# GpSimd's splits of the second weight block wait for the last low parts of the dense layer's input

## The chip, the cores and the metric

The kernel runs on one core of one Trainium2 chip. The metric is device time in microseconds (us) of one launch. In this text PE (TensorE) multiplies matrices, DVE (VectorE) and ACT (ScalarE) read its results from PSUM, POOL (GpSimd) works in SBUF only, and SP (SyncE) issues most of the DMAs. Each engine works through its own list of instructions in order, and waits on semaphores.

## The reference, cut to what matters

Four layers work on 4 x 256 tokens of 256 numbers, each followed by a residual sum and a layer norm: an mLSTM attention, a mixture of 16 experts of which each token takes 4, a gated linear attention (GLA) and a mixture of 32 experts of which each token takes 8. The change lies between the third and the fourth.

```python
x = _layernorm(x + _L1_attn_ref(x, ...))          # GLA, ends with silu(gproj) * o @ Wo.T
x = _layernorm(x + _L1_ffn_ref(x, ...))
# _L1_ffn_ref: routing and then every expert on every token
logits = x @ gate_weight.T
probs = softmax(logits); topv, topi = top_k(probs, 8)
...                                               # thresholds, then combine[token, expert]
gu = x @ w_gu.T; g, u = split(gu, 2)
acc = acc + (silu(g) * u) @ w_d.T * c_e[:, None]
```

## The kernel before

Products in full precision are made of three passes: each operand is split into a high part (a rounded copy) and a low part (the rest), and PE adds high times high, high times low and low times high (`mm3`, L1970). Tokens lie in 8 tiles of 128 (`NT`); two tiles share a PSUM bank, so there are 4 pairs.

**The dense layer.** The fourth layer computes all 32 experts for all tokens, in 8 blocks of 4 experts (`quad_slot(q)`). A block has six steps (`step_of`): two halves of 512 tokens, three chunks of 128 rows each. In a step PE makes the gate and the up product, 6 matmuls of 512 columns each (`gate_up`, L2299); ACT applies silu to the first (L1047) and in steps 0 to 5 copies the second to SBUF (L1052); the product of the two is made by POOL in steps 0 to 5 (`mixed`, L880) and by DVE later (L1677). Ten steps behind, POOL multiplies by the routing weights (L889), ACT and DVE split the product (L1070, L1682), and PE multiplies it by the down weights.

**The weights.** SP loads the gate, up and down weights of a block; POOL splits them: `high` (L811) and `low` (L816). Block 0 is split between the state products of GLA. Block 1 has its four splits in one piece after the last state product: a high and a low part of 1536 columns, then a high and a low part of 768 columns for the down weights. The first pair raises `gate_split` to 2, the second `down_split` to 2. They stand ahead of the six `mixed` products in POOL's list. PE needs `gate_split` 2 for step 6. SP waits for both before it loads block 3 (L589, L595), and after that for the routing weights.

**The input.** `lo_done` counts pairs whose low parts are written, four per layer. Its values 9 to 12 are the pairs of GLA's output before the projection `Wo` (`lo_parts`, L1549). Values 13 to 16 are the pairs of the normed sum, which is the dense layer's own input (`layernorm_by_halves`, DVE L1553, ACT L1005): per half of four tiles the statistics (L1559, L1567), `rv` = variance plus epsilon (L1569) and its reciprocal (L1570), ACT's root (L1010), the scaled tiles (DVE L1579, ACT L1013), four transposes per pair by PE (`turn_half`, L2247), the high parts by ACT (L1019) and the low parts by DVE (L1588).

**Where the routing stands.** PE begins step 0 with the first half's input (L2290, L2295), turns the second half, makes the router's products between the pieces of step 1 (L2256), and turns the logits (L2264). DVE then runs softmax, the eight best, the thresholds and the combine weights CW (`softmax` L1603, `route1` L1633, `combine` L1649) as one chain of some thirty small instructions from L1607 to L1665. PE turns CW (`turn_weights`, L2328) between steps 5 and 6, and step 7 waits until CW has been copied out of PSUM.

Around the change `AHEAD` is 6, and ACT's silu of step i waits for `mixed` of step i - 2, since both use two buffers:

```python
if 2 <= i < AHEAD + 2:
    act.wait_ge(mixed_pool, i - 1)
```

Of the kernel before, what the change touches and what calls it, by code (L numbers as in the profile page):

```python
# [28 lines left out]
def build_kernel(nc, a, out):  # L29
# [3 lines left out]
    NT = T // P  # L33
# [29 lines left out]
    with ExitStack() as ctx:  # L63
# [3 lines left out]
        def sem(name):  # L67
            return ctx.enter_context(nc.semaphore(name))
# [270 lines left out]
        lo_done = sem("lo_done")  # L339
# [147 lines left out]
        def quad_slot(q):  # L487


            n, c = GCOLS, DCOLS  # L490
            if q % 2 == 0:
                return [flat(EG[:])[:, 0:n], EW4[:, 0:n], EW4[:, n:2 * n],
                        flat(ED[:])[:, 0:c], EW4[:, 2 * n:2 * n + c], EW4[:, 2 * n + c:2 * n + 2 * c]]
            return [FA[:, 0:n], RA[:, 0:n], RA[:, n:2 * n],
                    FA[:, GLA_WORDS:GLA_WORDS + c], RA[:, 2 * n:2 * n + c], flat(W1H[:])[:, 0:c]]
# [52 lines left out]
        def _(sp):  # L548
# [15 lines left out]
            def load_expert(e, par):  # L564

                land_g, _, _, land_d, _, _ = MOE.slot(par)
                sp.dma_start(land_g.rearrange("p (k c) -> p k c", k=KD),
                             a["gateup0"][bass.ds(e, 1)].rearrange("o (k p) i -> p (o k) i", p=P)
                             ).then_inc(ld_exp[par], 16)
                sp.dma_start(land_d.rearrange("p (c d) -> p c d", d=D),  # L570
                             a["down0"][bass.ds(e, 1)].rearrange("o (c p) d -> p (o c) d", p=MOE.IP)
                             ).then_inc(ld_exp[par], 16)
# [68 lines left out]
        def _(pool):  # L641
# [195 lines left out]
                    low(dl, d, dh, whole, d_rounded).then_inc(down_split, 1)  # L837

            g, gh, gl, d, dh, dl = quad_slot(1)
            pool.wait_ge(lo_done, 3 * (NT // 2))  # L840
            pool.wait_ge(gate_ld[1], 32 * KD)
            g_rounded = high(gh, g, whole)
            low(gl, g, gh, whole, g_rounded).then_inc(gate_split, 1)
# [1119 lines left out]
        def _(pe):  # L1963
# [315 lines left out]
            def moe_pe():  # L2279

                def gate_up_first():

                    b = step_bank(0)
                    _, gh, gl, _, _, _ = quad_slot(0)
                    pe.wait_ge(gate_split, 1)
                    pe.wait_ge(hi_done, 3 * (NT // 2) + 2)
                    for up in range(2):
                        for k, (xh, _) in enumerate(xm(0)):
                            for j, g in enumerate((gh, gl)):
                                pe.matmul(bank(b + up), chunk_of(g, k, up, 0), xh, start=(k == 0 and j == 0), stop=False,  # L2290
                                          skip_group_check=True)
                    pe.wait_ge(lo_done, 3 * (NT // 2) + 2)
                    for up in range(2):
                        for k, (_, xl) in enumerate(xm(0)):
                            ins = pe.matmul(bank(b + up), chunk_of(gh, k, up, 0), xl, start=False, stop=(k == KD - 1),  # L2295
                                            skip_group_check=True)
                        ins.then_inc(gate_up_mm, 1)
# [382 lines left out]
```

## Time and profile before

| | us |
|---|---|
| median of 3 runs (lowest, highest) | 591.24 (590.7, 593.32) |
| the profiled execution | 589.8 |
| its span, first to last instruction | 588.0 |
| PE busy in the span | 523.6 (89%) |
| DVE, ACT, POOL busy | 327.0, 230.5, 348.8 |

The mean granted clock of TensorE in the span is 0.948 of full speed. A row of a timeline gives start, duration, engine, line, operation, the tiles written and read, and in brackets the idle time of the engine ahead of it with what ended it. Rows of one line that follow each other are merged (x4 is four instructions). A duration includes the time in which an instruction that has been started can't go on. L numbers are lines of the kernel.

### The profile page before, as it was taken

The numbers are of one execution on the slowest core, as the hardware profiler recorded it, in microseconds if no ns is written. First come the engines' busy times: TensorE is split into PE (matmuls) and PEld (weight loads), VectorE is DVE, ScalarE is ACT, GpSimd is POOL, SyncE is SP. The second block draws the span as 40 slices with busy tenths as digits, with TensorE's granted clock in tenths as the row PEclk, the third lists the DMA queues.
The fourth block names the chain that finished last, engine by engine and source line by source line (L and its number), as shares of the span: only waits on it lengthen the run. The fifth ranks groups of instructions, "written<-read, shape, count | busy, mean of one in ns | idle before, by whom it ended". The sixth has DMA issues, their size and how long they took to land.

```text
span 588.0 us, 9553 instructions
## 1 busy us (share of the span) xinstructions
PE 523.6 (89%) x3033; PEld 426.0 (72%) x3035; DVE 327.0 (56%) x726; ACT 230.5 (39%) x539; POOL 348.8 (59%) x316
## 2 busy tenths in 40 slices
PE   7999986339998999988989768999999999999994
PEld 4766666329887989966645438778888888888884
DVE  4635688634666444435998958563333252433276
ACT  3555542315554766545502022663232323232334
POOL 3394012777998797671377824254947657698180
PEclk9979998759998999999989968899999999999999
DMA  8999983245675766543000050204234343144022
GB/s 249 365 386 386 349 296 132 101 137 173 201 245 175 208 188 180 172 124 107 1 1 1 0 161 3 80 10 141 74 107 121 114 143 99 36 135 140 5 72 71
DMA packets 72864, 83.69 MB, mean 142 GB/s; under 512 B 7617, under 2 KB 63698, under 8 KB 72818
## 3 DMA queue, kind: packets, MB, share of 16 engines
q1 hardware_dynamic: 33490, 38.90, 22.0%
q10 hardware_dynamic: 35968, 35.26, 17.9%
q0 software_dynamic: 3360, 8.93, 4.9%
q8 instruction: 26, 0.43, 0.3%
q14 instruction: 20, 0.16, 0.1%
HBM read 48.61 MB, written 34.47 MB: 141 GB/s over the span
## 4 chain that ended last, share of the span: by engine, by line
PE 61%; DVE 14%; DMA 5%; issue 5%; POOL 4%; ACT 2%; ACTq 0%; DVEq 0%; POOLq 0%
PE PS L1970 47%; DMA FA<-xg 4%; POOL xg L708 3%; DVE FA L1923 2%; DVE PS L1904 2%; PE PS L2376 2%; PE PS L2495 2%; PE PS L2045 1%; PE PS L2067 1%; PE PS L2400 1%; PE PS L2507 1%; DVE HC L1378 1%; DMA FA<-yg,tix 1%; POOL FA L783 1%; PE PS L2192 1%
## 5 line engine op out<-in xcount | busy, mean ns | idle before, releaser
L1970 PE MATMUL PS<-XH,EW 128*128 128x512 f32 x392 | 129.8, 395 | 0.2 <-DVE EW L1278 0.2
L1677 DVE TENSOR_TENSOR FA<-OGATE,PS 128x512 f32<-128x512 f32 x42 | 28.9, 688 | 108.8 <-ACT OGATE L1047 90.7
L1970 PEld LDWEIGHTS PS<-XH,EW 128*128 128x128 f32 x392 | 73.7, 188 | 16.3 <-DVE EW L1278 0.7
L1970 PE MATMUL PS<-EW,XH 128*128 (+2 forms) x252 | 77.0, 389 | 3.6 <-issue 2.2
L1047 ACT ACTIVATE OGATE<-PS 128x512 f32<-128x512 f32 x48 | 28.7, 599 | 124.1 <-PE PS L1970 124.1
L1970 PE MATMUL PS<-XL,EW 128*128 128x512 f32 x196 | 77.0, 393 | 0.0
L1970 PE MATMUL PS<-EW 128*128 128x256 f32 x288 | 63.2, 284 | 0.6 <-DVE W1L L1682 0.4
L824 POOL TENSOR_TENSOR FA<-FA,QT 128x1024 f32<-128x1024 f32 (+1 forms) x16 | 37.4, 2338 | 32.5 <-DVE FA L1923 32.5
L1970 PE MATMUL PS<-EW,W1L 128*128 128x256 f32 x192 | 54.3, 283 | 0.0
L1970 PEld LDWEIGHTS PS<-EW 128*128 128x128 f32 x288 | 49.1, 189 | 4.2 <-DVE W1L L1682 1.5
L1970 PEld LDWEIGHTS PS<-EW,XH 128*128 128x128 f32 x252 | 44.8, 198 | 8.3 <-issue 2.8
L1682 DVE TENSOR_TENSOR W1L<-FA,EW 128x512 fp32r<-128x512 f32 x48 | 46.6, 978 | 2.8 <-ACT EW L1070 2.8
L1970 PE MATMUL PS<-EW,XL 128*128 (+2 forms) x126 | 46.6, 370 | 0.0
L889 POOL TENSOR_TENSOR FA<-FA,HC 128x512 f32<-128x512 f32 x24 | 34.5, 1442 | 16.7 <-DMA HC<-cw_room 16.7
L708 POOL DMA_INDIRECT xg<-XB,tix x32 | 31.3, 978 | 19.4 <-DVE tix L1463 10.4
L889 POOL TENSOR_TENSOR FA<-FA,QT 128x512 f32<-128x512 f32 x24 | 34.2, 1433 | 14.2 <-DMA QT<-cw_room 14.2
L1970 PEld LDWEIGHTS PS<-XL,EW 128*128 128x128 f32 x196 | 37.0, 189 | 6.8
L1970 PE MATMUL PS<-EW,EHH 112*128 x188 | 40.2, 306 | 0.1
L1923 DVE TENSOR_TENSOR_SCAN FA<-FA,PS 128x1024 f32<-128x1024 f32 x16 | 36.6, 2286 | 0.5
L1782 DVE TENSOR_TENSOR XL<-PS,XH 128x256 fp32r<-128x256 f32 x47 | 19.9, 424 | 30.0 <-ACT XH L1114 29.7
L1793 DVE TENSOR_TENSOR SQ<-SIL,PS 128x224 f32<-128x224 f32 x47 | 18.2, 388 | 32.7 <-ACT SIL L1133 32.2
L1970 PEld LDWEIGHTS PS<-EW,W1L 128*128 128x128 f32 x192 | 36.3, 189 | 0.0
(395 smaller groups left out, 1210.7 us busy)
## 6 DMA issues: line engine op xcount, KB each, us to landing
xg<-EQ ACTq DMA_DIRECT2D x1, 16384.0 KB, 60.7
EG<-in_gateup SPq DMA_DIRECT2D x16, 448.0 KB, 4.0
yg<-EQ ACTq DMA_DIRECT2D x1, 6016.0 KB, 19.7
FA<-xg ACTq DMA_DIRECT2D x47, 128.0 KB, 2.2
yg<-FA ACTq DMA_DIRECT2D x47, 128.0 KB, 2.6
ED<-in_down SPq DMA_DIRECT2D x16, 224.0 KB, 4.5
EG<-in_gateup SPq DMA_DIRECT2D x16, 192.0 KB, 3.0
FA<-in_gateup SPq DMA_DIRECT2D x16, 192.0 KB, 3.2
```

Of the source, the lines that this page charges most:

```text
L708: pool.indirect_dma_start(out=xg, out_offset=bass.IndirectOffsetOnAxis(ap=slots[:, n:n + 1], axis=0), in_=XB[:, t, :], in_offset=None).the ...
L824: pool.tensor_tensor(QS[:, v % 2, c], STATE[:, v % 2, c], QT[:, c], ALU.mult).then_inc(qs_done, 1)
L889: pool.tensor_tensor(mixed[:, v % MIXED, :], mixed[:, v % MIXED, :], spread_w[v % SPREADS], ALU.mult).then_inc(weighted, 1)
L1047: act.activation(sil_t[:, i % 2, :], bank(b), ACT.Silu).then_inc(sil_done, 1)
L1677: dve.tensor_tensor(mixed[:, i % MIXED, :], sil_t[:, i % 2, :], bank(step_bank(i) + 1), ALU.mult).then_inc(mixed_dve, 1)
L1682: dve.tensor_tensor(h_lo[:, v % TURNED, :], mixed[:, v % MIXED, :], h_hi[:, v % TURNED, :].bitcast(F32), ALU.subtract).then_inc(h_lo_done, 1)
L1782: dve.tensor_tensor(XL[:, :, c], bank(2 + i % 2)[:, 0:D].rearrange("p (k c) -> p k c", k=KD), XH[:, :, c].bitcast(F32), ALU.subtract).then ...
L1793: dve.tensor_tensor(HH[:, i % 2, 0:I], SIL[:, i % 2, 0:I], bank(i % 2)[:, I:2 * I], ALU.mult).then_inc(sh_ready, 1)
L1904: dve.tensor_tensor(spread_v(v), KT, spread_v(v), ALU.mult).then_inc(d1_done, 1)
L1923: dve.tensor_tensor_scan(STATE[:, v % 2, :], DEC, spread_v(v), 0.0, ALU.mult, ALU.add).then_inc(s_done, 1)
L1970: ins = pe.matmul(o, l, r, start=start and i == 0, stop=stop and i == n - 1, skip_group_check=True)
L2376: ins = pe.transpose(bank(2 + i % 2)[:, k * P:(k + 1) * P], XG[:, i % 4, k * P:(k + 1) * P], ident[:])
```

## The change

One number in POOL's list changes: the wait ahead of block 1's splits. Every engine has the same instructions in the same order as before.

```diff
@@ -837,7 +837,7 @@
                     low(dl, d, dh, whole, d_rounded).then_inc(down_split, 1)
 
             g, gh, gl, d, dh, dl = quad_slot(1)
-            pool.wait_ge(lo_done, 3 * (NT // 2))
+            pool.wait_ge(lo_done, 4 * (NT // 2))
             pool.wait_ge(gate_ld[1], 32 * KD)
             g_rounded = high(gh, g, whole)
             low(gl, g, gh, whole, g_rounded).then_inc(gate_split, 1)
```

`3 * (NT // 2)` is 12, the last pair of GLA's output; `4 * (NT // 2)` is 16, the last pair of the dense layer's input.

## Rows read from the trace of the kernel before

**Rows 1.** Chain of waits, 340 to 420 us: start, us, engine, tile, line

```profile
363.88 2.10 DVE rv L1569
...
380.48 0.70 DVE LG L1607
...
391.87 1.05 PE PS L2328 x8
392.91 27.17 PE PS L1970 x137
```

**Rows 2.** Timeline of POOL, 290 to 405 us

```profile
360.89 1.48 POOL L811 TENSOR_SCALAR EW<-FA 128x1536 fp32r<-128x1536 f32 x1 [16.48 <-DVE XL L1549]
362.46 3.49 POOL L816 TENSOR_TENSOR EW<-FA,EW 128x1536 fp32r<-128x1536 f32 x1
...
366.83 1.81 POOL L816 TENSOR_TENSOR W1H<-FA,EW 128x768 fp32r<-128x768 f32 x1
379.66 2.56 POOL L880 TENSOR_TENSOR FA<-OGATE 128x512 f32<-128x512 f32 x2 [11.01 <-ACT OGATE L1052]
385.58 1.29 POOL L880 TENSOR_TENSOR FA<-OGATE 128x512 f32<-128x512 f32 x1 [3.36 <-ACT OGATE L1052]
387.07 1.29 POOL L880 TENSOR_TENSOR FA<-OGATE 128x512 f32<-128x512 f32 x1 [0.21 <-ACT OGATE L1052]
```

**Rows 3.** Timeline of DVE, 370 to 425 us

```profile
370.84 0.17 DVE L1569 TENSOR_SCALAR rv<-mv 128x4 f32<-128x4 f32 x1
...
375.39 1.42 DVE L1588 TENSOR_TENSOR XL<-PS,XH 128x256 fp32r<-128x256 f32 x4 [2.82 <-ACT XH L1019]
...
381.21 0.42 DVE L1610 TENSOR_REDUCE rsum<-LG 128x8 f32<-128x256 f32 x1
...
385.13 0.22 DVE L1635 TENSOR_TENSOR t<-t,alpha 128x64 f32<-128x64 f32 x1
...
385.65 1.31 DVE L1637 TENSOR_TENSOR t<-t,rsum 128x64 f32<-128x64 f32 x1
...
387.50 0.88 DVE L1642 SCALAR_TENSOR_TENSOR rbest<-rsum,rbest 128x8 f32<-128x8 f32 x1
```

**Rows 4.** Timelines of DVE and POOL later in the dense layer, 414 to 420 us

```profile
414.39 2.54 POOL L889 TENSOR_TENSOR FA<-FA,HC 128x512 f32<-128x512 f32 x2
...
415.99 1.49 DVE L1682 TENSOR_TENSOR W1L<-FA,EW 128x512 fp32r<-128x512 f32 x1
416.90 2.29 POOL L816 TENSOR_TENSOR EW<-FA,EW 128x768 fp32r<-128x768 f32 x1
```

**Rows 5.** Timeline of PE, 345 to 425 us

```profile
367.81 1.06 PE L2247 MATMUL PS<-ident,XB 128*128 128x128 f32 x8 [1.89 <-DVE XB L1579]
369.70 3.30 PE L2290 MATMUL PS<-XH,EW 128*128 128x512 f32 x8 [0.83 <-ACT XH L1019]
...
380.37 0.50 PE L1970 MATMUL PS<-XH,EW 128*128 128x512 f32 x1
...
391.39 0.39 PE L1970 MATMUL PS<-XH,EW 128*128 128x512 f32 x1
```

**Rows 6.** Windows: length, busy of five engines, TensorE's granted clock, DMA share, GB/s

```profile
182.50:189.30 6.80, 4.64 (x20) 4.36 (x21) 4.09 (x8) 1.93 (x6) 4.88 (x7) 0.75 0.51 161
325.80:332.60 6.80, 4.28 (x18) 1.54 (x17) 6.73 (x5) 0.00 (x0) 5.29 (x4) 1.00 0.00 0
...
366.80:373.60 6.80, 4.96 (x18) 3.97 (x19) 5.32 (x19) 4.19 (x8) 1.81 (x1) 0.75 0.60 174
```

**Rows 7.** Timeline of ACT, 370 to 425 us

```profile
372.74 1.28 ACT L903 ACT_TABLE_LOAD   x1
...
374.75 1.09 ACT L1019 ACTIVATE XH<-PS 128x512 fp32r<-128x512 f32 x2 [0.52 <-PE PS L2247]
...
384.37 0.58 ACT L1047 ACTIVATE OGATE<-PS 128x512 f32<-128x512 f32 x1
```

**Rows 8.** Timeline of SP's DMA issues, 340 to 420 us

```profile
365.98 2.50 SPq L589 DMA_DIRECT2D FA<-in_gateup  x4
```

## The prediction

> **What bounds the kernel now.** I read the page first: PE is busy for 89% of the span. Then the chain of waits over the end of GLA and the start of the dense layer. From 392.9 us on it is one row of 137 matmuls and stays on PE [rows 1]. So what counts is the time at which PE can go on from the turned routing weights, 391.87. Whatever moves that instant moves the end by as much, and a wait in the front of the chain counts only as far as it reaches it.
>
> Ahead of it the chain goes through two pieces of DVE. The first is the layer norm of the first half: `rv` (L1569), four numbers per partition, takes 2.10 us [rows 1], and its twin for the second half 0.17 [rows 3]. The timeline of POOL shows what stands beside it: the low split of block 1, 362.46 plus 3.49, ends at 365.95, and `rv` ends at 365.97 [rows 1, 2]. DVE waited for the end of a POOL instruction. The second piece is the routing chain, L1607 at 380.48 to CW, ready just ahead of 391.87. It shows the same three times: L1637 takes 1.31 us where L1635, of the same form, takes 0.22, and ends at 386.96, beside a POOL product that ends at 386.87; L1642 takes 0.88 and ends at 388.38, beside one that ends at 388.36 [rows 2, 3]; L1611 in the same way waits for the end of the pair of products from 379.66. These three hold some 1.1, 0.7 and 0.4, together 2.2 us. L1610, a reduction of one tensor, runs in 0.42 in the middle of a POOL product and isn't held [rows 2, 3]. So instructions of DVE that read two tensors from SBUF, and small ones like `rv`, are held to the end of POOL's current instruction; reads of PSUM and reductions are not.
>
> PE itself was nearly as late as CW: its last matmul of step 5 starts at 391.39 and its turn of CW at 391.87, so 0.2 us were spare [rows 1, 5]. Both arms have to get shorter for a gain.
>
> **The change, step 1: the stall goes.** POOL is then silent from GLA's last product until the last low part. `rv` falls from 2.10 to 0.17, which is 1.9 us on the chain. PE waited 1.89 for that half's tiles ahead of 367.81 [rows 5], so it can take all of it and start turning at some 365.9.
>
> **Step 2: the clock.** In the 6.8 us from 366.8 on the granted clock averages 0.75: half of the stretch is at 1.2 GHz [rows 6]. The 8 matmuls of step 0 take 3.30 us there. At 2.4 GHz the 48 matmuls of steps 2 to 5 start over 391.39 - 380.37 = 11.02 us, 0.234 each [rows 5], so eight take 1.9. Ahead of the fall PE stood still for 1.89 and 0.83 us; the first of the two goes. I take it that the clock then stays up here, worth 1.4 for the 8 and some 0.3 for the 4 after them. Not all arrives: ACT's table load ends at 374.02, and its high part at 374.75, which had waited 0.52 for PE, comes behind it [rows 7]. That row can move by 1.9 for the stall and by 0.5 for the wait at most, to 372.3. The last low part, at 376.81 before [rows 3], keeps its distance of 2.1 and comes at 374.4. From there PE has 4 router matmuls and 6 of step 1, 10 x 0.234 = 2.3, and the turn of the logits, eight small transposes, for which I take 0.7 (the eight of CW's turn take 1.05 [rows 1]): L1607 starts at 377.5 in place of 380.48, a lead of 3.0 us. If the clock falls all the same, the lead is 1.9.
>
> **Step 3: the splits now stand in front of the routing chain.** Before they took 360.89 to 368.64, 7.75 us [rows 2]. Now: high part 374.4 to 375.9, low part to 379.5, the down weights' high part to 380.3, their low part to 382.2. Queued behind them are the six products. The first began at 379.66 before [rows 2]; now it can't begin before 382.2, so the first two run to 383.5 and 384.8. ACT's silu of step 2 waits for the first of them. It ran at 384.37 before, late because of the routing's table loads [rows 7], now at 383.6. PE's step 4 waits for that silu: it would be there at 377.4 + 24 x 0.234 = 383.0 and starts at 384.2. It still reaches the turn of CW at 384.2 + 24 x 0.234 = 389.8, 1.8 ahead of before.
>
> DVE's chain is worse off, because POOL is now busy without a gap from 374.4 to 384.8 and then nearly without. I walk it with the durations of before and hold each two-tensor instruction to the end of the POOL instruction then running: L1611 waits 0.5 (low part), L1620 0.6 (down low), L1623 0.9 (first product), L1635 1.1 (second), L1637 0.8 (third), L1639 1.1 (fourth), L1642 1.1 (fifth), L1663 0.2 (sixth): 6.3 us in place of 2.2. One DVE instruction goes in between two POOL instructions in a row: L1682 started inside a pair of POOL products, and took 1.49 until 417.48; the POOL instruction after the pair then took 2.29 [rows 4] where the same form takes 1.81 [rows 2]. If DVE had no turn in between, the chain would wait for a gap in POOL's work, up to 2 us more. The nearest row says that it gets its turn, and I take that. What holds eight instructions up is a matter of tenths: an instruction ready just ahead of POOL's next one isn't held at all, and each such escape gives 0.8 to 1.1 back.
>
> CW's instant: 391.87 - 3.0 (lead) + 6.3 - 2.2 (holds) = 393.0, **1.1 us later than before**. PE, there at 389.8, stands still for some 3 us.
>
> The Trainium skill, "SBUF — State Buffer", section "SBUF: two separate sides", says that GpSimd and a VectorE instruction that uses both its read ports share one pair of ports as an exclusive lock: whoever starts first has it for the whole instruction, the other fully blocks. The holds above agree. No row here has the eight MAX8 of L1614 beside POOL; by that page's rule they, with one input, aren't held, and the sum stays; if they were, a part of 0.8 would be added.
>
> **Step 4: PE's pause.** Two stretches that held a pause lost half their clock: 182.5 to 189.3, busy 4.64 of 6.80, and 366.8 to 373.6. A third, 325.8 to 332.6, busy 4.28, kept it [rows 6]. A single pause of 3 us with PE busy to both sides is closest to the first. I give the fall 6 in 10 where PE waits so long, at the price of the stretch at 370: 1.4 us. Bounds: 0 and 1.7.
>
> **Other edges.** PE needs the split for step 6, after 392.9; it is done at 379.5. SP's loads of block 3, issued at 365.98 before, start at 379.5 and end near 383; its next work waits for the copy of CW, which PE turns at 391.87 before, so that costs nothing [rows 1, 8]. The cover is some 9 us thick. POOL's sixth product follows PE's step 5 as before.
>
> **The sum.** +1.1 (CW) + 1.4 (clock) = +2.5 us on the profiled execution, 589.8 to 592.3. That execution lies 1.4 under the median of the runs; on the median it is 593.7, or 0.4% up: by that less than the 0.5% which a measurement of this kernel can tell from no change.
>
> **The rivals.**
> A. The same, and the clock stays up at 390: +1.1, 592.3. For it: the third stretch of [rows 6].
> B. The chain slips through. Holds stay near the 2.2 of before, since ready times fall into POOL's seams; then CW leads, PE's arm decides, 391.6 to 389.8, -1.8 us: 589.4. Against it: POOL has hardly a seam before 384.8. Over 0.5% faster would take -3, which not even PE's arm gives.
> C. Slower: the clock still falls at 370, so the lead is 1.9 and not 3.0. The last low part comes at 374.9, the splits end at 382.7, CW at 391.87 - 1.9 + 4.1 = 394.1, +2.2, or +1.4 if the later start spares L1611 and L1639 a part of their holds; with the fall after it +3.6: 594.8. It decides from a CW over 1.6 later than before together with the fall.
> D. The stall of `rv` has nothing to do with POOL: no lead, all the holds: +4.1, 595.3. The coinciding ends speak against it.
>
> **How the numbers follow.** Forecast 0.42, A 0.22, B 0.16, C 0.16, D 0.04. The likeliest is 593.7. Its own spread is some 1 us, so a quarter of its chance (0.10) lies beyond 594.2, where 0.5% ends; with C's larger part and D that makes slower 0.26. Faster by 0.5% needs under 588.3: 0.04, from B. Within: 0.70. The range takes in B's centre and C's: 589.4 to 595.2.
>
> **What the profile of the changed kernel would show.** Right: the first `rv` at some 0.17; the splits from 374.4; granted clock 1.0 from 366 to 374; L1607 at about 377.5; a silu of step 2 released by POOL's product; L1620 to L1642 at about 1 us each; PE's idle time ahead of L2328 near 3 us with DVE named, and a stretch at half clock behind it. Wrong: `rv` still long (step 1), half clock at 370 (step 2), L1607 to L1665 hardly longer than the 11.3 of before (step 3), full clock after the pause (step 4).

## The result, and the profile after

| | before | changed |
|---|---|---|
| median us (lowest, highest) | 589.49 (584.18, 596.59), 20 runs | 593.84 (587.5, 598.59), 20 runs |
| the profiled execution | 589.8 | 587.76 |

The ratio is 1.0066, with an interval of 1.0039 to 1.0092: 0.7% slower, by some 3.9 us. The medians are of all 20 runs, while the ratio leaves out runs over 1.5% above the fastest of their kernel, of which the changed kernel has 3. Timed a second time beside the experiments the ratio was 1.0057 (1.0023 to 1.009). The profiled execution of the changed kernel is one of the fastest of its 20, so its span of 585.9 against 588.0 says nothing by itself. Clock and history ahead of this place differ between executions by several us. So all instants below that are called "from L1355" count from the start of DVE's instruction L1355, the first of the norm inside GLA. It lies 9.7 us ahead of the splits of the kernel before, the first thing that the change moves. In these two executions it starts at 351.21 and 347.67.

The timeline of DVE before, and that of the changed kernel:

```profile
351.21 0.29 DVE L1355 TENSOR_SCALAR hs<-PS 128x128 f32<-128x128 f32 x1 [3.35 <-PE PS L2547]
...
381.66 0.84 DVE L1611 TENSOR_TENSOR LG<-LG,rsum 128x256 f32<-128x256 f32 x1
382.98 0.85 DVE L1614 MAX8 top<-PR 128x8 f32<-128x32 f32 x8 [0.48 <-ACT PR L1034]
...
391.39 0.42 DVE L1665 TENSOR_TENSOR CW<-CW,rsum 128x256 f32<-128x256 f32 x1
```

```profile
347.67 0.29 DVE L1355 TENSOR_SCALAR hs<-PS 128x128 f32<-128x128 f32 x1 [3.35 <-PE PS L2547]
...
360.34 0.17 DVE L1569 TENSOR_SCALAR rv<-mv 128x4 f32<-128x4 f32 x1
...
373.85 0.69 DVE L1607 TENSOR_REDUCE LG<-PS 128x256 f32<-128x512 f32 x1 [3.27 <-PE PS L2264]
...
375.03 0.96 DVE L1611 TENSOR_TENSOR LG<-LG,rsum 128x256 f32<-128x256 f32 x1
376.48 0.85 DVE L1614 MAX8 top<-PR 128x8 f32<-128x32 f32 x8 [0.48 <-ACT PR L1034]
...
377.93 0.71 DVE L1620 SCALAR_TENSOR_TENSOR rv<-rsum,rbest 128x8 f32<-128x8 f32 x1
...
378.91 1.03 DVE L1623 TENSOR_TENSOR t<-top,rsum 128x64 f32<-128x64 f32 x1
379.97 1.19 DVE L1635 TENSOR_TENSOR t<-t,alpha 128x64 f32<-128x64 f32 x1
...
381.45 1.09 DVE L1637 TENSOR_TENSOR t<-t,rsum 128x64 f32<-128x64 f32 x1
382.58 0.23 DVE L1639 TENSOR_TENSOR t<-t,first 128x64 f32<-128x64 f32 x1
...
383.10 0.88 DVE L1642 SCALAR_TENSOR_TENSOR rbest<-rsum,rbest 128x8 f32<-128x8 f32 x1
...
384.54 1.27 DVE L1647 TENSOR_TENSOR t<-top,t 128x64 f32<-128x64 f32 x1
...
387.53 1.25 DVE L1663 SCALAR_TENSOR_TENSOR CW<-HC,PR 128x256 f32<-128x256 f32 x1
388.81 0.93 DVE L1665 TENSOR_TENSOR CW<-CW,rsum 128x256 f32<-128x256 f32 x1
```

The stall of the first `rv` is gone: 0.17 in place of the 2.10 of [rows 1]. L1607 starts 26.2 from L1355, against 29.3 in [rows 1]. From there on the chain loses what it had won. L1623 and L1635 take over 1 us each; [rows 3] has L1635 with POOL idle, 0.22. An instruction is called held here where it takes longer than its form does with POOL idle: 0.42 for two inputs of 128x256, 0.22 for 128x64, 0.17 for 128x8. Nine instructions are held, together 6.8 us. Before it was 2.3, of which three instructions (L1611, L1637, L1642) make 2.2. CW is ready at 42.1 from L1355 in place of 40.6.

The timelines of POOL and ACT in the changed kernel show what stands beside the chain:

```profile
370.66 1.47 POOL L811 TENSOR_SCALAR EW<-FA 128x1536 fp32r<-128x1536 f32 x1 [28.92 <-DVE XL L1588]
372.22 3.49 POOL L816 TENSOR_TENSOR EW<-FA,EW 128x1536 fp32r<-128x1536 f32 x1
...
376.77 1.84 POOL L816 TENSOR_TENSOR W1H<-FA,EW 128x768 fp32r<-128x768 f32 x1
378.57 3.90 POOL L880 TENSOR_TENSOR FA<-OGATE 128x512 f32<-128x512 f32 x3
382.67 1.29 POOL L880 TENSOR_TENSOR FA<-OGATE 128x512 f32<-128x512 f32 x1 [0.20 <-ACT OGATE L1052]
```

```profile
379.95 0.60 ACT L1047 ACTIVATE OGATE<-PS 128x512 f32<-128x512 f32 x1 [1.99 <-POOL FA L880]
```

The splits follow the last low part, and three products follow the splits without a gap; before, the first two products stood alone and the third came 3.4 us later [rows 2]. ACT's silu of step 2 now waits 1.99 for a product of POOL. The timeline of PE in the changed kernel:

```profile
364.11 2.11 PE L2290 MATMUL PS<-XH,EW 128*128 128x512 f32 x8 [0.83 <-ACT XH L1019]
```

```profile
380.60 0.50 PE L1970 MATMUL PS<-XH,EW 128*128 128x512 f32 x1 [0.99 <-ACT OGATE L1047]
...
386.06 0.40 PE L1970 MATMUL PS<-XH,EW 128*128 128x512 f32 x1
...
389.80 1.05 PE L2328 MATMUL PS<-ident,CW 128*32 128x128 f32 x8 [3.33 <-DVE CW L1665]
```

The eight matmuls of step 0 run at full clock, 2.11 us for the 3.30 of [rows 5]. Step 4 waits 0.99 for the silu. And PE, done with step 5, stands still for 3.5 us until CW is there; before it hardly waited. The 3.5 counts from 386.3, when a next matmul could have started (0.23 behind the last one); the 3.33 in the brackets counts from the recorded end of the last one. All pauses of PE below are counted in the first way, except where brackets are named.

From the turn of CW (the start of L2328) to the end, called the tail below, it is 196.10 us in this execution and 196.13 in that of before. So between these two executions all the difference in this part is the instant of the turn: 42.13 from L1355 against 40.66. That makes the changed kernel 1.5 us slower here; its span is shorter all the same, because L1355 starts 3.5 us earlier in this execution.

### The profile page after: what moved, and what is told of

The parts are those of the page before. It is cut to its first block, busy times and chain, and to the rows that moved or that the text cites. A ratio compares the mean times of both kernels' runs of the same rounds, so it can differ in the third digit from the quotient of the medians.

```text
span 585.9 us, 9553 instructions
## 1 busy us (share of the span) xinstructions
PE 520.2 (89%) x3033; PEld 421.4 (72%) x3035; DVE 329.3 (56%) x726; ACT 230.3 (39%) x539; POOL 348.1 (59%) x316
## 4 chain that ended last, share of the span: by engine, by line
PE 56%; DVE 14%; POOL 6%; DMA 6%; issue 4%; ACT 3%; POOLq 1%; ACTq 0%; SPq 0%; DVEq 0%
PE PS L1970 44%; DVE FA L1923 3%; DMA FA<-xg 2%; DMA FA<-yg,tix 2%; DVE PS L1904 2%; POOL FA L783 2%; DMA ED<-in_down 2%; POOL xg L708 2%; PE PS L2495 1%; PE PS L2045 1%; PE PS L2067 1%; PE PS L2376 1%; PE PS L2507 1%; PE PS L2400 1%; POOL EW L752 1%
## 5 line engine op out<-in xcount | busy, mean ns | idle before, releaser
L811 POOL TENSOR_SCALAR EW<-FA 128x768 fp32r<-128x768 f32 (+1 forms) x11 | 11.2, 1027 | 50.4 <-DVE XL L1588 28.9
L1970 PE MATMUL PS<-EW,EHH 112*128 x188 | 39.6, 303 | 0.1
```

The lines of the kernel that those rows point to most:

```text
L1970: ins = pe.matmul(o, l, r, start=start and i == 0, stop=stop and i == n - 1, skip_group_check=True)
```

## The experiments

Each diff below is against the changed kernel. Two theories stood against each other at first. H: the loss is made by POOL's splits ahead of the routing chain (a later CW), and by the clock, which falls in some executions after PE's pause. R: it comes from elsewhere (the wait itself, the later loads of block 3, or something that every kernel with a silent POOL would pay). The profiled instants are a sharper measure than the medians here, whose intervals are some 0.3% wide to each side.

| kernel | turn of CW from L1355 | turn to end | holds | ratio to before |
|---|---|---|---|---|
| before, three profiles | 40.66, 39.60, 39.60 | 196.1, 196.3, 196.4 | 2.3 | 1 |
| changed, four profiles | 42.13, 42.15, 42.15, 42.17 | 196.1, 199.1, 198.0, 196.4 | 6.8 | 1.0066, 1.0057 |
| pause filled (e2) | 42.12 | 196.3 | 6.8 | 1.0054 |
| gate pair early, down pair at the last low part (e3) | 39.92 | 198.0 | 4.6 | 0.9985 |
| splits of 16 columns (e4) | 37.57 | 196.2 | 2.3 | 0.9987 |
| all splits at the scaled tiles (e5) | 39.95 | 198.0 | 4.6 | 1.0018 |
| gate pair early, down pair at the scaled tiles (e6, e8) | 37.57, 37.61 | 196.4, 196.1 | 2.3 | 0.9978, 0.9959 |
| gate pair as before, down pair late (e7) | 39.75 | 196.1 | 2.6 | one run |

### The changed kernel three times more (e1, c1, c2)

No edit.

> The changed kernel again, beside the kernels of this set. Theory H (holds and clock): CW, the combine weights, is ready about 1.5 us later than before; PE pauses about 3.3 us ahead of turning it (L2328), and in a part of the executions the clock falls to 1.2 GHz after the pause, some 1.4 us more. Ratio to before 1.003 to 1.007. Rival N (the first count of runs was noise, and the profiled execution, 2 us faster than that of before, is typical): ratio 0.997 to 1.001.

> The changed kernel, a third profile, for what varies between its executions. Theory H: CW turned at 42.1 after L1355 as in the first two; the time from there to the end 196.1 to 196.4 if the clock stays up, 198 to 199.1 if it falls at the pause of 3.5 us; I expect the fall in more than half of the executions. Rival (the fall of the second profile was an exception): 196.1 to 196.4.

> The changed kernel, a fourth profile, with the same two outcomes: 42.1 to the turn, then 198 to 199.1 with a fall of the clock at the pause (theory H, more than half of the executions) or 196.1 to 196.4 (rival).

Measured: 1.0057 (1.0023 to 1.009), so N, that the first count of runs was noise, falls. The turn stands at 42.1 to 42.2 in all four profiles; it is no accident of one execution. What varies is the tail. In two of four it is 196.1 and 196.4, in c1 198.0, in e1 199.1. The timelines of e1, DVE and then PE, and its windows (length, busy of five engines, granted clock, DMA share, GB/s):

```profile
348.28 0.29 DVE L1355 TENSOR_SCALAR hs<-PS 128x128 f32<-128x128 f32 x1 [1.72 <-PE PS L2547]
```

```profile
390.43 1.89 PE L2328 MATMUL PS<-ident,CW 128*32 128x128 f32 x8 [3.34 <-DVE CW L1665]
```

```profile
384.00:388.00 4.00, 3.10 (x14) 2.19 (x12) 3.86 (x23) 2.75 (x6) 2.06 (x3) 1.00 0.00 0
388.00:392.00 4.00, 1.57 (x9) 1.10 (x9) 2.31 (x3) 0.22 (x1) 3.92 (x3) 0.67 0.00 0
392.00:396.00 4.00, 4.00 (x12) 3.12 (x11) 0.68 (x1) 1.18 (x2) 0.04 (x1) 0.50 0.15 33
396.00:400.00 4.00, 4.00 (x18) 3.26 (x17) 0.87 (x2) 0.60 (x1) 1.65 (x2) 0.98 0.62 186
```

PE had been at full clock and mostly busy until 387, then paused; the clock falls to 1.2 GHz still within the pause and stays there for 6.8 us. The turn of CW takes 1.89 in place of 1.05, and the tail is 2.9 us longer. In c1 the low stretch lasts 3.4 us and costs 1.7. The fall came in 2 of 4 executions where I had expected more than half.

### PE's pause filled (e2)

```diff
-                    pe.wait_ge(cw_step, CW_READY)
                     pe.wait_ge(sil_done, AHEAD - 1)
                     pe.wait_ge(up_copied, AHEAD - 1)
+                    keep_warm(12, 2)
+                    pe.wait_ge(cw_step, CW_READY)
```

> The changed kernel, with 12 matmuls on zeros (128x512 bf16, bank 2, which the turned weights overwrite) ahead of PE's wait for CW, so that PE is busy for some 2.6 of the 3.3 us of its pause. CW's time is not touched. Theory H: what is left is the later CW, +1.5 us or less; the share of the clock goes, so ratio 1.000 to 1.003, below the changed kernel of this set by 1 to 2.5 us. Rival C (the clock plays no part, all of the loss is the later CW): same as the changed kernel within 0.5 us.

The timeline of PE in e2:

```profile
389.81 2.54 PE L1992 MATMUL PS<-zb 128*128 128x512 bf16 x11
393.08 1.05 PE L2329 MATMUL PS<-ident,CW 128*32 128x128 f32 x8 [0.73 <-DVE CW L1665]
```

The idle time ahead of the turn shrinks to 0.73, the clock stays up, the turn is where it was. The times don't decide: 1.0054 (1.0025 to 1.0083) against 1.0057 for the changed kernel in the same set. The medians are 592.3 and 592.95 us, 0.65 apart, where each interval is 1.7 to 2 us wide to each side. So the fall of the clock is shown by profiles, its share in the median is not shown by this run. And 1.0054 is more than the 1.5 us that I had left for the later CW. That contradiction led to the next question: is the profile of before typical?

### The kernel before twice more (b1, b2)

No edit.

> The kernel before, a second profile, to see which parts of the first one vary between executions. Theory P (where the clock stays up at 370 us in that kernel, CW is turned earlier): rv about 2.1, CW turned at 40.7 after L1355 if the clock falls there, and 39.5 to 40.2 if it doesn't. Rival: 40.7 in both.

> The kernel before, a third profile, with the same question: 40.7 after a fall of the clock at 370 us, 39.5 to 40.2 without one (theory P), or 40.7 in both.

The timelines of DVE and PE in b1:

```profile
350.27 0.29 DVE L1355 TENSOR_SCALAR hs<-PS 128x128 f32<-128x128 f32 x1 [3.35 <-PE PS L2547]
...
378.48 0.69 DVE L1607 TENSOR_REDUCE LG<-PS 128x256 f32<-128x512 f32 x1 [3.27 <-PE PS L2264]
```

```profile
389.87 1.05 PE L2328 MATMUL PS<-ident,CW 128*32 128x128 f32 x8
```

L1607 stands at 28.2 and the turn at 39.6, in both; the clock stayed up around 370. Theory P holds: the half clock of [rows 6] at 366.8 to 373.6 is there in one of three executions and costs 1.1 us. The change therefore moves CW from a usual 39.6 to 42.1, by 2.5 us, not by 1.5. With the tails of e1 and c1 (2.9 and 1.7, none in two, so 1.1 on the average) and 0.4 for the one execution of before in three that was late, this gives 2.5 + 1.1 - 0.4 = 3.2 us, against 3.4 to 3.9 measured. The averages are of four profiles and of three, so this agreement is rough. With e2's tail it gives 2.1, or 1.0036, inside its interval.

### Splits of 16 columns (e4)

```diff
+            bit = lambda w: w[:, 0:16]
-            g_rounded = high(gh, g, whole)
-            low(gl, g, gh, whole, g_rounded).then_inc(gate_split, 1)
+            g_rounded = high(gh, g, bit)
+            low(gl, g, gh, bit, g_rounded).then_inc(gate_split, 1)
...
```

> The changed kernel with the four splits of block 1 cut to 16 columns each: the waits and counts stay, POOL's 7.8 us of work go (so the weights of block 1 are left unsplit, a part of the computation that this kernel leaves out). Theory H: lead of 3.0 at L1607, holds of 2 to 2.5 us in the routing chain, CW about 2.5 to 3 us earlier than before, PE's pause under 0.5: ratio 0.994 to 0.996. Rival R: the wait itself, or the loads of block 3 that start later, cost the time: ratio 1.003 or more as in the changed kernel.

This kernel leaves out the splits of the other columns of block 1, so its result is not that of the reference. The turn of CW stands at 37.57, 4.6 us ahead of the changed kernel, with the wait as it is there. The holds are 2.3, those of before, and PE has no pause. So the wait by itself costs nothing, and the 7.8 us of splits in that place make all of the 4.5 us of additional holds. SP's loads of block 3 are not quite where the changed kernel has them: they are issued 23.5 us from L1355, against 28.1 there and 14.8 before. That the later loads cost nothing is shown by the time from the turn to the end, 196.1 in the changed kernel with its loads latest of all, and 196.2 here. So theory R falls for the wait and for the loads. The ratio, 0.9987 (0.995 to 1.0024), has its middle above the 0.994 to 0.996 expected. These had been counted from the late profile of before; the turn is 2.0 us ahead of a usual one, which is 0.9966, inside the interval.

### The gate pair early, the down pair late (e3)

```diff
             g, gh, gl, d, dh, dl = quad_slot(1)
-            pool.wait_ge(lo_done, 4 * (NT // 2))
+            pool.wait_ge(gated, 2 * NT)
             pool.wait_ge(gate_ld[1], 32 * KD)
...
+            pool.wait_ge(lo_done, 4 * (NT // 2))
             pool.wait_ge(down_ld[1], 16)
```

> The splits are parted: the gate pair (high and low, 5.1 us) starts as soon as DVE has scaled GLA's output (16 more counts of gated), about 2.8 us earlier than before, so that it ends ahead of the first rv (L1569); the down pair (2.7 us) waits for the last low part, as in the changed kernel. Theory H: rv 0.17 us, the second rv and L1607 lead as in the changed kernel (2.7 to 3.1 us ahead of before), the down pair ends ahead of the first product of POOL that ACT needs, the holds in the routing chain fall back to 2 to 3.5 us in place of 6.9, CW 1.5 to 3 us earlier than before, PE's pause under 0.5 us: ratio 0.994 to 0.998. Rival R (what made the changed kernel slower is not the splits' place ahead of the routing chain): ratio 1.002 or more. A third outcome: the gate pair is itself slowed or slows DVE's last scaling, rv still waits: ratio 1.000.

The first `rv` takes 0.17 and L1607 comes at 26.2, as expected; CW doesn't: the turn is at 39.9, just where a usual execution of before has it. The down pair itself is over at 25.75 from L1355, ahead of the chain. But POOL's first two products queue behind it and start 0.37 us later than in e6 (below), at 25.72 against 25.35. The second of them holds L1611 (L1612 in these kernels) by 0.36 us more. That alone shifts the chain by 0.36, and L1658, near its end, then starts 0.03 us behind the start of a POOL product that it escapes in e6: 1.12 us. L1666, late by both, runs into the next product: 0.94. The timeline of POOL in e3, and then those of DVE in e3 and in e6:

```profile
377.29 2.52 POOL L881 TENSOR_TENSOR FA<-OGATE 128x512 f32<-128x512 f32 x2
...
387.06 1.29 POOL L881 TENSOR_TENSOR FA<-OGATE 128x512 f32<-128x512 f32 x1 [1.09 <-ACT OGATE L1053]
```

```profile
378.93 1.16 DVE L1612 TENSOR_TENSOR LG<-LG,rsum 128x256 f32<-128x256 f32 x1
...
387.09 1.27 DVE L1658 SCALAR_TENSOR_TENSOR rsum<-rv,rsum 128x8 f32<-128x8 f32 x1
...
390.06 1.37 DVE L1666 TENSOR_TENSOR CW<-CW,rsum 128x256 f32<-128x256 f32 x1
```

```profile
380.28 0.80 DVE L1612 TENSOR_TENSOR LG<-LG,rsum 128x256 f32<-128x256 f32 x1
...
388.11 0.15 DVE L1658 SCALAR_TENSOR_TENSOR rsum<-rv,rsum 128x8 f32<-128x8 f32 x1
...
390.02 0.43 DVE L1666 TENSOR_TENSOR CW<-CW,rsum 128x256 f32<-128x256 f32 x1
```

A late start of 0.36 us came out as 2.3 us of later CW, and the holds are 4.6 where 2 to 3.5 were expected. The pause of PE is 2.6 us here, and the clock fell behind it (a tail of 198.0). By this profile the kernel would be 0.3 + 1.7 - 0.4 = 1.6 us slower than before, 1.0027. Its measured ratio is 0.9985 (0.995 to 1.002), below that; whether the clock falls in fewer of its executions isn't shown.

### All splits at the scaled tiles (e5)

```diff
-            pool.wait_ge(lo_done, 4 * (NT // 2))
+            pool.wait_ge(x_dve, NT)
```

> All four splits wait until DVE has scaled the second half's tiles (x_dve 8), 3.4 us ahead of the last low part. Between the two DVE has only its low parts, which read PSUM. Counted from DVE's L1355 of the GLA norm. Theory H (the loss comes from splits and products beside the routing chain): splits from 19.4 to 27.2, L1607 at 26.2 as in the changed kernel, holds 2.3 to 3.3 us in place of 6.8, CW turned at 37.6 to 38.8 (before 40.7, changed 42.1), PE's pause under 1.5: ratio 0.995 to 1.000. Rival O (all kernels that silence POOL in the norm carry a further 2 us of something else): ratio 1.000 to 1.003 in spite of a CW 2 us earlier.

The turn is at 39.95, more than 1 us beyond what I had expected, again with a pause of 2.6 and a fall behind it. The splits end at 27.2 as planned; but the products then start beside L1611 (0.96 held), and the late chain meets two more of them, at L1657 (0.90 held) and at L1665 (0.95 held). With the two holds of before that is 4.6 us, as in e3. The timeline of DVE in e5, whose L1355 starts at 355.48:

```profile
382.88 1.38 DVE L1611 TENSOR_TENSOR LG<-LG,rsum 128x256 f32<-128x256 f32 x1
...
391.27 1.05 DVE L1657 SCALAR_TENSOR_TENSOR rsum<-rv,rsum 128x8 f32<-128x8 f32 x1
...
394.01 1.37 DVE L1665 TENSOR_TENSOR CW<-CW,rsum 128x256 f32<-128x256 f32 x1
```

The ratio is 1.0018 (0.9989 to 1.0047).

### The gate pair early, the down pair at the scaled tiles (e6, e8)

```diff
-            pool.wait_ge(lo_done, 4 * (NT // 2))
+            pool.wait_ge(gated, 2 * NT)
...
+            pool.wait_ge(x_dve, NT)
             pool.wait_ge(down_ld[1], 16)
```

> The gate pair starts when GLA's output is scaled (gated 16), the down pair when the second half's tiles are scaled (x_dve 8). Theory H: no split stands beside the routing chain, holds 2.3, CW turned at 37.6 as with splits of 16 columns, no pause of PE: 3.1 us ahead of the profiled execution of before, ratio 0.994 to 0.998. Rival O: ratio 0.998 to 1.001 as with splits of 16 columns (0.9987).

> The kernel with the gate pair at gated 16 and the down pair at x_dve 8, timed a second time, since its first interval (0.9948 to 1.0008) takes in 1. Theory H: CW turned at 37.6, 2.0 us ahead of the usual execution of before (39.6) and 3.1 ahead of one in which the clock fell: 2.0 to 2.4 us on the average, ratio 0.996. Rival O (a further loss of some 2 us eats the gain): ratio 0.999 to 1.001.

The timelines of POOL and PE in e6, whose L1355 starts at 352.93:

```profile
359.97 1.48 POOL L811 TENSOR_SCALAR EW<-FA 128x1536 fp32r<-128x1536 f32 x1 [12.96 <-DVE HC L1379]
361.53 3.51 POOL L816 TENSOR_TENSOR EW<-FA,EW 128x1536 fp32r<-128x1536 f32 x1
372.32 0.83 POOL L811 TENSOR_SCALAR EW<-FA 128x768 fp32r<-128x768 f32 x1 [7.29 <-DVE XB L1580]
373.24 1.85 POOL L816 TENSOR_TENSOR W1H<-FA,EW 128x768 fp32r<-128x768 f32 x1
378.28 2.52 POOL L881 TENSOR_TENSOR FA<-OGATE 128x512 f32<-128x512 f32 x2 [3.18 <-ACT OGATE L1053]
```

```profile
390.50 1.05 PE L2329 MATMUL PS<-ident,CW 128*32 128x128 f32 x8
```

Each pair lies where DVE's tensors come from PSUM, wholly or as one of two inputs: the gate pair beside GLA's low parts and the statistics, ended before the first `rv`, the down pair beside the second half's low parts, ended 3.2 us before the first product. The turn is at 37.6 in both profiles, as with 16 columns. The ratio was 0.9978 (0.9948 to 1.0008) and, the second time, 0.9959 (0.9925 to 0.9993). Both intervals lie below that of the changed kernel. Against the kernel before, one of the two excludes 1; the 2.0 us by which the turn is earlier (0.34%) are inside both. This is the best version that I found.

### The gate pair as before, the down pair late (e7)

```diff
-            pool.wait_ge(lo_done, 4 * (NT // 2))
+            pool.wait_ge(lo_done, 3 * (NT // 2))
...
+            pool.wait_ge(lo_done, 4 * (NT // 2))
             pool.wait_ge(down_ld[1], 16)
```

> The gate pair waits as in the kernel before (lo_done 12), the down pair as in the changed one (lo_done 16). Theory H, counted from L1355: the first rv is stalled again (about 2.1 us), L1607 at 28.2 (29.3 if the clock falls), the down pair ends at 27.7 to 28.8, ahead of the routing chain; holds 2.3 to 2.8, CW turned at 39.6 to 40.1 (or one more with the fall): the down pair costs nothing in its new place, all of the loss comes from the gate pair's 5.1 us. Rival: the down pair alone already pushes POOL's products, holds over 4, CW turned at 41 or later.

`rv` is stalled for 2.03 again, L1607 stands at 28.1, CW is turned at 39.75: 0.15 later than in a usual execution of before. The timelines of POOL and DVE in e7:

```profile
389.47 1.33 POOL L881 TENSOR_TENSOR FA<-OGATE 128x512 f32<-128x512 f32 x1 [1.13 <-ACT OGATE L1053]
```

```profile
389.48 0.16 DVE L1658 SCALAR_TENSOR_TENSOR rsum<-rv,rsum 128x8 f32<-128x8 f32 x1
```

In this order the down pair's place is nearly free, in the one profile there is. But that hangs on hundredths: L1658 started 0.01 us behind POOL's product here and wasn't held, and 0.03 behind it in e3, where it was held for 1.12. So what a pair costs can't be told by itself. Counted from the order of e6, the down pair beside the chain costs 2.3 us (e3), and the gate pair with it 4.6 (the changed kernel). The expectation that all of the loss comes from the gate pair holds for the order of e7 alone.

## Why the prediction was right and wrong

The time lay inside the range, and the mechanism was the one forecast. But 0.7% is above the 0.5% within which I had put seven chances of ten; slower by more than that had 0.26. That the likeliest time, 593.7, is almost the measured median of 593.84 is luck: it was counted up from 591.24, the median of three runs of before, and twenty runs put that kernel at 589.49. As a change, 0.7% stands against the 0.4% forecast.

**Step 1, the stall goes: right.** 0.17 for `rv`, and PE turns its tiles without the wait of 1.89 that [rows 5] shows.

**Step 2, the lead: right as an instant, wrong as a gain.** Forecast: clock up, last low part 2.1 behind ACT's high part, L1607 3.0 us earlier. Measured: clock up, 2.0 behind, and 3.1 earlier than in [rows 1]. But the two other profiles of before have L1607 at 28.2 with the clock up. The half clock at 370 that I took for part of the kernel is there in one of three profiles. Over a usual execution the lead is 2.0 us. This is the step that failed, and it is worth 1.1 us of the 3.9. I had moreover counted the gain on from the median of runs, though two of the three profiles never had that loss.

**Step 3, the holds: right within 0.5 us in sum, which is partly luck, since not by the same instructions.** Forecast 6.3, measured 6.8. L1611, L1620, L1623, L1635, L1637 were held as walked (0.5, 0.5, 0.8, 1.0, 0.9). L1639 escaped (0.0 for 1.1) since it was ready 0.1 us ahead of POOL's fourth product; L1642 was held 0.7 for 1.1; L1647 was held in its place (1.05), and L1663 and L1665 together 1.3 in place of 0.2. The claim that DVE has its turn between two POOL instructions held: L1623 and L1635 ended behind the first and the second of three products in a row. CW's turn was forecast at 393.0, which is 41.8 from L1355, and came at 42.1. Step 4's wait for the silu was forecast as 1.2 and was 0.99.

The rule of the Trainium skill, "SBUF — State Buffer", "SBUF: two separate sides", of an exclusive lock, is also borne out for what it doesn't take in: L1614's eight MAX8 took 0.85 us in the changed kernel beside the down pair, and 0.85 in the kernel before with POOL idle. They have one input, so by that page they aren't held, and they weren't.

**Step 4, the pause: right in kind, too cheap.** 3.5 us of pause for 3; a fall in 2 of 4 executions for 6 in 10; 1.7 and 2.9 us for the 1.4 forecast. I had taken the price from a stretch of 3.4 us, and in e1 it was twice that long.

**The sum.** +1.1 and +1.4 were forecast. Measured against a usual execution: +2.5 for CW, some +1.1 on the average for the clock. Rival A is what two of the four profiles show. C had the right side of 0.5%, but not its reason: the clock at 370 didn't fall in the changed kernel, it had fallen in the profile of before. B and D fell.

## What to carry to other kernels

A wait that protects one short chain moves the work behind another: before moving GpSimd work, list the VectorE instructions in its new place that were seen to be held (those with two SBUF inputs, and here also the small `tensor_scalar` of L1569 from SBUF to SBUF), each of which can wait for the rest of the GpSimd instruction then running, and look for places where VectorE works from PSUM, as e6 does. A delay of a few tenths in such a chain can come out as 2 us, and in e3 and e7 a few hundredths decide over 1 us, so the order of ready times has to be read, not the sum of the work. And a loss of clock in one profile is a property of that execution until a second one shows it: take two or three profiles before a gain is counted on it.

## What was not expected of the hardware

The granted clock after a pause of 3.5 us in PE's work: unchanged in two executions of four, at 1.2 GHz for 3.4 us in one and for 6.8 us in another, which cost 1.7 and 2.9 us. With pauses of 2.6 us (2.4 by the brackets) it fell in both profiles there are (e3, e5; tails of 198.0). With the pause filled to 0.73 (by the brackets) it didn't fall, in one profile.
